# Projecting packed halves of the images with fp32r products, with a new order on all engines of a ViT tower kernel

## The reference, cut to what matters

```python
# x: (16 images, 64 channels, 256 positions, 4 heads) fp32
y = einsum('nclh,dc->ndlh', x, w) + b          # for q, k, v: D = 64, flattened to (n, 256, 256)
ew = exp(w_bias * local_mask)
num = einsum('ts,nsd->ntd', ew, exp(k) * v)
den = einsum('ts,nsd->ntd', ew, exp(k))
h = layernorm((sigmoid(q) * num / den) @ out_w + out_b + flatten(x)) * ln_g + ln_b
h = concatenate([cls_tok, h])                  # 257 rows per image
h = h + gated_recurrence(layernorm(h))         # gates r, i; scan along the rows; W_out
h = h + moe(layernorm(h))                      # shared FFN 256-1024-256 + top 2 of 8 experts
```

## Time and profile before

| | |
|---|---|
| runs | 1001.1, 1001.7, 1005.56 us (median 1001.7) |
| profiled execution | 1007.98 us, span 1006.3 us |
| mean granted TensorE clock | 0.961 |
| TensorE busy | 946.8 us (94%) |
| VectorE, ScalarE, GpSimd busy | 675.8, 458.2, 380.8 us |
| instructions | 21535 |

### The profile page before, as it was taken

The page is one execution under the profiler, slowest core; times in us unless marked ns, Lnnn a source line. Parts: engine busy times, 40 slices in busy tenths (PEclk is TensorE's granted clock), DMA queues, the critical chain, the costliest instruction groups (busy, mean ns, idle before and its releaser), DMA issues.

```text
span 1006.3 us, 21535 instructions
## 1 busy us (share of the span) xinstructions
PE 946.8 (94%) x6825; PEld 887.4 (88%) x6825; DVE 675.8 (67%) x2091; ACT 458.2 (46%) x1132; POOL 380.8 (38%) x470
## 2 busy tenths in 40 slices
PE   6979999999999999999886799999999999999996
PEld 4768899888898888898785799999999999999996
DVE  3588878887788877779777355654646456554643
ACT  2214344443444443444232355555555555555553
POOL 5282433333433424324524235342423435352322
PEclk9779999999999999999979799999999999999998
DMA  9315111001111001100013626473362825464222
GB/s 267 135 30 154 43 43 43 21 21 42 42 42 38 16 30 42 42 32 22 23 36 137 212 43 174 91 202 57 73 183 42 215 50 122 138 162 103 45 42 32
DMA packets 48163, 82.71 MB, mean 82 GB/s; under 512 B 6415, under 2 KB 30881, under 8 KB 48130
## 3 DMA queue, kind: packets, MB, share of 16 engines
q0 software_dynamic: 31056, 57.46, 23.7%
q1 hardware_dynamic: 17074, 24.83, 8.3%
HBM read 55.34 MB, written 26.96 MB: 82 GB/s over the span
## 4 chain that ended last, share of the span: by engine, by line
PE 60%; issue 19%; POOL 8%; DVE 7%; DMA 2%; ACT 1%; POOLq 1%; SPq 1%; DVEq 0%
PE ps_nd L755 17%; PE ps_proj L739 14%; PE ps_ri L739 6%; PE ps_nd L917 5%; PE ps_proj L822 5%; POOL out L700 5%; PE ps_ip L739 4%; PE ps_h L905 3%; PE ps_ip L890 2%; PE ps_t L829 2%; DMA R<-v_rows 1%; PE ps_t L1226 1%; DVE rden L1757 1%; DVE E L1750 1%; DVE yb L1984 1%
## 5 line engine op out<-in xcount | busy, mean ns | idle before, releaser
L1579 DVE TENSOR_TENSOR GL<-g_act,GH 128x256 fp32r<-128x256 f32 (+1 forms) x416 | 170.6, 423 | 169.8 <-ACT GH L1280 168.3
L1275 ACT ACTIVATE g_act<-ps_proj,fcb 128x256 f32<-128x256 f32 (+1 forms) x272 | 129.5, 476 | 284.9 <-PE ps_proj L739 264.0
L755 PE MATMUL ps_nd<-w2h,GH 128*128 128x256 f32 x832 | 240.9, 290 | 2.1 <-DVE GL L1579 2.1
L755 PE MATMUL ps_nd<-w2h,GL 128*128 128x256 f32 x832 | 233.9, 281 | 0.0
L755 PE MATMUL ps_nd<-w2l,GH 128*128 128x256 f32 x832 | 233.1, 280 | 0.0
L755 PEld LDWEIGHTS ps_nd<-w2h,GH 128*128 128x128 f32 x832 | 156.5, 188 | 6.3 <-issue 1.6
L1280 ACT CAST GH<-g_act 128x256 fp32r<-128x256 f32 (+1 forms) x416 | 161.0, 401 | 1.1
L755 PEld LDWEIGHTS ps_nd<-w2l,GH 128*128 128x128 f32 x832 | 157.1, 189 | 0.0
L755 PEld LDWEIGHTS ps_nd<-w2h,GL 128*128 128x128 f32 x832 | 156.5, 188 | 0.0
L739 PE MATMUL ps_proj<-xh,w1h 128*128 128x256 f32 (+1 forms) x544 | 127.8, 317 | 13.4 <-DVE E L1750 8.7
L700 POOL DMA_INDIRECT out<-yb,rows_to x72 | 115.5, 1605 | 16.7 <-issue 14.0
(11 more groups left out here) (263 smaller groups left out, 1844.1 us busy)
## 6 DMA issues: line engine op xcount, KB each, us to landing
R<-v_rows SPq DMA_DIRECT2D x37, 260.0 KB
w1h<-fc_w POOLq DMA_DIRECT2D x9, 1024.0 KB, 7.0
w2h<-pj_w POOLq DMA_DIRECT2D x9, 1024.0 KB, 9.8
stage<-fc_w POOLq DMA_DIRECT2D x9, 1024.0 KB, 11.7
stage<-pj_w POOLq DMA_DIRECT2D x9, 1024.0 KB, 14.0
v_rows<-tail_rows SPq DMA_DIRECT2D x16, 260.0 KB, 3.0
x<-x SPq DMA_DIRECT2D x16, 256.0 KB, 3.5
out<-yb SPq DMA_DIRECT2D x16, 256.0 KB, 2.2
```

The costliest lines, as they stand in the source:

```text
L755: last = pe.matmul(banks[a], g[:, j, a * P:(a + 1) * P], w[i][:, j, :], start=(j == 0 and q == 0), stop=(j == HT - 1 and q == 2))
L1275: act.activation(g_act[:, j % G_SLOTS, 0:width], banks[j % len(banks)][:, 0:width], ACT.Gelu_apprx_tanh, bias=fcb[i][:, j:j + 1]).then_inc ...
L1579: dve.tensor_tensor(GL[:, j, 0:width], g_act[:, j % G_SLOTS, 0:width], GH[:, j, 0:width].bitcast(F32), ALU.subtract).then_inc(gl_done, 1)
```

## The change

For images 2 to 15 the projection is computed from halves. x is laid out head by head as fp32r. `XA` has 128 rows: rows 0 to 63 the high part of x, rows 64 to 127 its low part. `XB` has 97 rows: the high part of x, then rows of ones. `WA` holds the high weights twice, `WB` the low weights, then zeros, then the high bias row. One product of XA with WA and one of XB with WB, accumulated in the bank, replace one fp32 product. ScalarE makes the high parts in two copies per image (`x_high`), VectorE the low part in one subtraction (`x_low`); SP loads x twice, into rows 0 to 63 and 64 to 127 of `X[par]`. XA, XB, WA, WB and `wproj_h` lie in buffers of expert 1's weights (`W1L[1]`, `W2L[1]`, `W1H[1]`, `W2H[1]`), so `next_weights` moves from step 2 to step 16 of GpSimd and waits for the last projection. Four loads (`pack_weights`), three copies (`pack_fill`) and one subtraction (`pack_split`) prepare the weights at the start.

Besides: `ranks` uses three products; the tails are written in step 18 of the mixer by SP, two blocks behind each list's end after image 14, and `rows_out` of image 15 waits for them; every engine but GpSimd and VectorE reads its limits before the experts' first block; eight products (`WARM`) stand before the first transpose of the experts, and `spare` adds 16 fp32 products in the start. The loop holds five pairs (images 4 to 13); steps 14 and 15 are written out as well, and the order of the calls is new in all written-out steps and in `step` of TensorE, ScalarE, VectorE and GpSimd.

```diff
+    KB = 97
-        X = [sb(f"x{i}", [KA, LH]) for i in range(2)]
+        X = [sb(f"x{i}", [P, LH]) for i in range(2)]
+        XA = [W1L[1][:].rearrange("p k n -> p (k n)")[:, i * LH:(i + 1) * LH] for i in range(2)]
+        XB = [W2L[1][:].rearrange("p j m -> p (j m)")[0:KB, i * LH:(i + 1) * LH] for i in range(2)]
+        WA = W1H[1][:, 0, :]
+        WB = W1H[1][0:KB, 1, :]
...
 load_x (SP)
-                after(sp, proj_ready, LT * (n - 1))
+                packed = not isinstance(n, int) or n >= 2
+                if isinstance(n, int) and n < 4:
+                    after(sp, proj_ready, LT * (n - 1))
+                else:
+                    sp.wait_ge(xs_done, n - 3)
                 sp.dma_start(X[par][0:C, :], x[n]).then_inc(x_loaded[par], 16)
+                if packed:
+                    sp.dma_start(X[par][C:2 * C, :], x[n]).then_inc(x_loaded[par], 16)
...
+            def tails(t, par):
+                sp.wait_ge(ends_ready, 1)
+                for e in range(NE):
+                    end = sp.value_load(ends_i[0:1, e:e + 1], min_val=e * LIST,
+                                        max_val=e * LIST + TOK - BLK)
+                    sp.dma_start(v_rows[bass.ds(end, 2 * BLK), :]
+                                 .rearrange("(b p a) m -> p b a m", b=2, a=2),
+                                 tail_rows[:].unsqueeze(1).to_broadcast([P, 2, 2, W])
+                                 ).then_inc(tails_stored, 16)
...
 GpSimd
+            def pack_weights(t, par):
+                flat_w = w_proj.rearrange("c h d -> c (h d)")
+                pool.dma_start(wproj_h, flat_w).then_inc(pack_loaded, 16)
+                pool.dma_start(WA[0:C, :], flat_w[0:C, :]).then_inc(pack_loaded, 16)
+                pool.dma_start(WA[C:2 * C, :], flat_w[0:C, :]).then_inc(pack_loaded, 16)
+                pool.dma_start(WB[KB - 1:KB, :], flat_w[C:KA, :]).then_inc(pack_loaded, 16)
             def next_weights(t, par):
+                pool.wait_ge(proj_ready, LT * NIMG)
             def step(t, par):
                 rstd_h(t, par)
                 affine(t, par)
+                rstd_u(t, par)
                 rstd_v(t, par)
-                rstd_u(t, par)
+                rows_out(t, par)
                 out_bias(t, par)
-                rows_out(t, par)
...
 project (TensorE)
                 for h in range(H):
-                    last = pe.matmul(ps_proj[:, h, :], head_view(par, lt, h), wproj[:, h, :],
-                                     start=True, stop=True)
+                    if packed:
+                        cols = slice(h * 4 * D, (h + 1) * 4 * D)
+                        pe.matmul(ps_proj[:, h, :], packed_view(XA[par], lt, h), WA[:, cols],
+                                  start=True, stop=False)
+                        last = pe.matmul(ps_proj[:, h, :], packed_view(XB[par], lt, h),
+                                         WB[:, cols], start=False, stop=True)
...
 ranks (TensorE)
-                for lt in range(LT):
-                    for k in range(lt + 1):
-                        pe.matmul(ps_rank[:, lt, :], (before_r if k == lt else ones_r)[:],
-                                  rmask[:, k, :], start=(k == 0), stop=(k == lt))
-                for k in range(LT):
-                    last = pe.matmul(ps_tot, ones_r[:], rmask[:, k, :], start=(k == 0),
-                                     stop=(k == LT - 1))
-                last.then_inc(rank_ready, 1)
+                pe.matmul(ps_count, ones_r[:], rmask_z[:].rearrange("p t e -> p (t e)"),
+                          start=True, stop=False)
+                pe.matmul(ps_count[:, 0:LT * NE], before_r[:],
+                          rmask.rearrange("p t e -> p (t e)"), start=False, stop=False)
+                pe.matmul(ps_tot, ones_r[:], rmask[:, 0, :], start=False, stop=True
+                          ).then_inc(rank_ready, 1)
...
+            def spare(t, par, k):
+                pe.wait_ge(consts, CONSTS)
+                for _ in range(2):
+                    pe.matmul(ps_ri[:, 1, :], ones_pp[:], zeros[:, 0, :], start=True, stop=True)
...
 step (TensorE)
                 hidden(t, par, 0)
+                hidden(t, par, 1)
                 sums0(t, par)
-                hidden(t, par, 1)
+                hidden(t, par, 2)
                 sums1(t, par)
-                hidden(t, par, 2)
                 hidden(t, par, 3)
+                hidden(t, par, 4)
                 turn_u(t, par)
-                hidden(t, par, 4)
+                hidden(t, par, 5)
                 rank(t, par)
-                hidden(t, par, 5)
+                hidden(t, par, 6)
                 gates0(t, par)
+                input0(t, par)
+                hidden(t, par, 7)
                 turn_v(t, par)
-                hidden(t, par, 6)
-                input0(t, par)
                 gates1(t, par)
...
 experts_tensor
+            limits = block_limits(pe)
+            for _ in range(WARM):
+                pe.matmul(ps_t[:, 0, :], ones_r[:], W2H[0][:, 0, :], start=True, stop=True)
             transpose_rows(0)
...
 ScalarE
+            def x_high(t, par):
+                n = t + 1
+                if live(n):
+                    p = 1 - par
+                    act.wait_ge(x_loaded[p], 16 * (n - p) + 16)
+                    if not isinstance(n, int) or n >= 4:
+                        act.wait_ge(proj_ready, LT * (n - 1))
+                    act.copy(XA[p].rearrange("c (h l) -> c h l", h=H),
+                             X[p][:].rearrange("c (l h) -> c h l", h=H)).then_inc(xq_done, 1)
+                    act.copy(XB[p][0:C, :].rearrange("c (h l) -> c h l", h=H),
+                             X[p][0:C, :].rearrange("c (l h) -> c h l", h=H)).then_inc(xq_done, 1)
 step (ScalarE)
                 gelu_j(t, par, 0)
                 gelu_j(t, par, 1)
                 high(t, par, 0)
+                x_high(t, par)
                 gelu_j(t, par, 2)
+                high(t, par, 1)
                 gelu_j(t, par, 3)
-                high(t, par, 1)
-                copy_u(t, par)
                 high(t, par, 2)
                 gelu_j(t, par, 4)
-                tanh0(t, par)
+                copy_u(t, par)
...
 VectorE
-                    if isinstance(n, int) and n == NIMG - 1:
-                        dve.wait_ge(run_ready, NIMG + 1)
+                    if isinstance(n, int) and n == NIMG - 2:
+                        dve.wait_ge(run_ready, NIMG)
                         dve.tensor_copy(ends_i[:], run[:]).then_inc(ends_ready, 1)
+            def x_low(t, par):
+                n = t + 1
+                if live(n):
+                    p = 1 - par
+                    dve.wait_ge(xq_done, 2 * (n - 1))
+                    low = XA[p][C:2 * C, :].rearrange("c (h l) -> c h l", h=H)
+                    dve.tensor_tensor(low, X[p][C:2 * C, :].rearrange("c (l h) -> c h l", h=H),
+                                      low.bitcast(F32), ALU.subtract).then_inc(xs_done, 1)
 step (VectorE)
                 ekv0(t, par)
                 h_sum(t, par)
+                ekv1(t, par)
                 h_norm(t, par)
-                ekv1(t, par)
...
                 u_norm(t, par)
-                ratio0(t, par)
-                u_low(t, par)
-                v_norm(t, par)
                 low(t, par, 0)
                 low(t, par, 1)
-                ratio1(t, par)
-                y_last(t, par)
+                v_norm(t, par)
+                u_low(t, par)
                 low(t, par, 2)
-                places(t, par)
+                ratio0(t, par)
                 low(t, par, 3)
                 low(t, par, 4)
+                ratio1(t, par)
+                places(t, par)
                 low(t, par, 5)
+                v_low(t, par)
                 low(t, par, 6)
+                x_low(t, par)
                 slots_out(t, par)
-                v_low(t, par)
+                y_last(t, par)
+                low(t, par, 7)
                 gate_a(t, par)
-                low(t, par, 7)
                 gate_b(t, par)
                 base_sum(t, par)
```

728 lines of the change are left out of this document (483 added, 245 removed).

## The result

The change makes the kernel slightly slower. Eight runs of the changed kernel have a median of 1011.2 us (1004.2 to 1017.9), beside 1006.1 us (1001.1 to 1006.9) of the kernel before on the same chip: ratio 1.0058, 95% interval 1.0032 to 1.0083. The forecast was 964 us, in a range of 944 to 986. The forecast was counted down from 1001.7 us, the median of three runs of the kernel before; the median of eight is 4.4 us higher, which would move the forecast by as much and no more. The profiled execution has a span of 1012.7 us, 6.4 more than the profiled one of before.

A forecast was written before the change was run, and what follows sets the result against it. TensorE, busy 94% of the span, was taken as the bound, with VectorE able to close in. Savings of 23 (twelve steps), 3 (start) and 12 (tail), 38 us, took the 1001.7 us median to 964 us; range 944 to 986.

The forecast's parts named there:

- the lower ends: Helper prices per image: x_high on ScalarE 2.24 of 2.24 to 3.7 us, x_low on VectorE 1.23 of 1.23 to 2.0.
- rival 1: Loop: added strided work becomes the bound, factor 1.65 on both helpers, 16 us over twelve steps, 980 us; chance 0.20.
- "nothing" for the load of x: SP queue: the second load of each x, 256 KB more per step, waits for x_low two images back; costs nothing.
- rows_out ahead of out_bias: GpSimd: the new order puts H0 off by 5 us, but v_sum wants it 8 us after next turn_y; costs nothing.
- the products: TensorE: 8 fp32r products replace each fp32 projection, 0.94 us together, saving 1.82 us per step; 2.05 with ranks.
- 28.9 us was laid out: Loop: one new step takes 28.9 us instead of 30.8, saving 1.9; twelve steps give 23 us.
- 3 faster forecast: Start: gains from projections and no next_weights, less spares and helpers; 3 us faster, between 8 slower and 12 faster.
- 12 forecast: Tail of the mixer: tails and limits moved earlier, next_low_second, new order of last steps; 12 us faster, between 5 and 20.
- stand in the wait for R: Tail: the eight WARM products cost nothing unless R is already there, then under 2 us.
- The 2.2 us for next_low_second: Tail: next_low_second leaves the stretch where it held VectorE's yb sum, worth 4.4 us, counted half: 2.2 us.
- Rival 4: Loop: strided reading costs ScalarE and VectorE factor 2.5, 4.3 us more per step, 52 in all, 1016 us; chance 0.04.
- signs for wrong: Copies of 1.9 us or more; hidden 4 or last ffn_out waiting over 1 us; GpSimd idle on a DMA; image 4 after 105 us.

The follow-up runs named there:

- e4: Changed kernel with input x laid out head by head by the host, so helpers and weight loads read at unit stride, all other work kept: 989.1 us median.
- e7: Changed kernel with SyncE issuing the load of image t+1 ahead of base_out(t): 6.7 us less than the changed kernel by the medians, ratio 0.9974.
- e8: Changed kernel with GpSimd adding out_bias ahead of rows_out in the loop's steps, as before the change: 2 us gained by the medians.
- e5: Changed kernel's order with the fp32 projection for all images, one load of x, no helpers or weight packing: ratio interval 0.9956 to 1.001 to the kernel before.
- e16: Changed kernel; from image 5 ScalarE gathers x once, halves and x_low read that copy packed; SyncE loads image t+1 early: 988.2 us, ratio 0.9862 to kernel before.
- e15: Changed kernel; from image 5 ScalarE gathers x once and halves and x_low read that copy packed; no early load: ratio interval 0.9939 to 1.0005 to kernel before.
- e9: Changed kernel with x_high and x_low packed in the order of x, TensorE's projection weight loads reading at a stride of 4 elements instead: 1015.6 us.
- e11: Changed kernel with both the head-by-head input of e4 and SyncE's early load of e7: 993 us.
- e10: e9 plus SyncE's early load of image t+1 ahead of base_out(t): worse still than e9, time not given.
- e13: Changed kernel; from image 4 ScalarE gathers x once into a free buffer, halves and x_low read that copy packed; no early load: 1014 us median.

## Why the prediction was wrong

**The step that failed is the pricing of x_high and x_low**: "I take the lower ends, since the same operation on the same engine is a nearer row than another engine's load or a reduction." The nearer row lacked the one property that decides, the stride. Both rows that had it said 1.6 to 1.65; measured are 1.95 on ScalarE and 1.65 on VectorE, 1.85 and 0.8 us more per image. The Trainium skill, "Advanced Engine Details and Errata", section "SBUF Cachelines", tells of a penalty where each access meets a different line; it pointed the right way, and these runs supply the price. The upper ends of the range, 3.7 and 2.0 us, were nearly right, but even they were taken too lightly: rival 1 had 16 us for them. The runs put the stride at 2.0 us a step between e4 and the changed kernel, and at 22 us by the medians (1011.2 against 989.1). That is about half of the miss: even with packed reads the kernel takes 989 us, above the range. Of the 44 us by which the profiled execution misses the sum, 22.5 lie in the twelve steps, 11.5 in the start and 11.4 in the tail, and the experts give 1.0 back; the points below have the rest.

**Second, "nothing" for the load of x.** "On SP nothing urgent is queued behind that wait, only base_out": the queue was read in one direction. base_out waits for VectorE's last operation of the step, and the next image's load is queued behind it. e7 gives it 1.0 us a step in the changed kernel, and 3.9 us in step 14. It cost nothing visible in e4's loop, where ScalarE and VectorE had room. The prediction also laid out one step and took it twelve times, and steps 14 and 15 have orders of their own.

**Third, rows_out ahead of out_bias: "nothing".** H0 was not late (in the ten steps VectorE waits 0.7 us in all for GpSimd, for rstd); but out_bias moved beside VectorE's sum, 1.95 us for 0.69 in four steps of ten. Undoing it moved the collision and gained 2 us by the medians (e8), no more than their spread.

**Right: the products.** A projection's 8 records stand 0.12 us apart (328.43 to 329.47 us, 1.04 in all where the sum had 0.94), the wider weights cost nothing, and with packed helpers the ten steps give 25.4 us in e4's profile where the sum had 19: 28.9 us was laid out and 28.3 came. The surplus fits the clock: before, every second step was at 0.95 and 1.5 us longer, in e4 none. The prediction took the pair's mean as given and did not ask whether it would change.

**Start: 3 faster forecast, 8.5 slower measured**, just past the bound of 8. The order alone has 4.8 of it (e5), and e4's start is 3 to 6 shorter than those of the changed kernel and its equals, which is the stride's part, the packed weight loads of images 0 and 1 included; both are near what equal starts differ by. VectorE and ScalarE have the chain there (start us, us, what):

```profile
31.36 1.98 ACT w2l L1561 x2
...
33.37 2.04 ACT w1l L1550
35.41 1.95 ACT w2l L1552
...
37.38 0.06 DVE w1l L2218
37.44 2.54 issue
39.98 1.22 DVE w1h L2225
41.20 0.67 DVE st L1821 x2
```

The "issue" here is x_low at work: its one operation runs from 37.38 us for 2.57. pack_fill, x_high, x_low and pack_split stand ahead of u_stats, which began at 36.57 us before and at 41.20 now. The prediction had these durations as VectorE's load and not as a chain.

**Tail: 12 forecast, 0.6 measured.** Tails left SyncE's path as said, and from the last sum to the experts' first product it is 12.6 us where it was 17.1. From the start of the tail to that sum it is 72.1 us where it was 68.1, which takes most of it back. What is late behind the sum was not only the last scatter:

```profile
555.36 0.69 DVE yb L2210
...
557.53 0.18 DVE bounds L2515
557.71 5.89 issue
563.60 2.07 PE ps_t L1396 x8
565.67 0.87 PE ps_t L1368 x4
```

VectorE writes the counts after its last sum, TensorE then takes 5.9 us to read eight limits (the prediction had 3.35 from the earlier trace rows, the part that stood on the chain there) and starts the WARM products at 563.60, while R had landed before 561.47, when VectorE copied from it (timeline):

```profile
561.47 0.17 DVE L2531 COPY info<-R 128x8 f32<-128x8 f32 x1 [0.89 <-DMA R<-v_rows]
```

That the WARM products "stand in the wait for R" was wrong: they lie behind the limits. In the same chain of before R was the last thing that the transposes waited for. The 2.2 us for next_low_second did not come either: it still holds a sum of yb, which is on the chain for 4.40 us where it was 5.08 (chain, and timeline of GpSimd):

```profile
540.15 4.40 DVE yb L2210
```

```profile
539.27 4.73 POOL L530 TENSOR_TENSOR w2l<-stage,w2h 128x1024 fp32r<-128x1024 f32 x2
```

By order alone the end gains 5.2 us (e5). In the changed kernel steps 14 and 15 take 3.9 us longer than in e5 and what follows up to the last sum 4.4, and that loses it again; how much of the 4.4 is the helpers isn't shown.

Of the rivals, rival 1, strided helpers at 1.65, had the mechanism and the step: 28.9 and 1.35 us make 30.25, and 30.3 came, though from 28.3 and 2.0. Its 980 us failed by steps 14 and 15, the start and the tail. Rival 4 had the sign and nearly the number (1016 us), at 0.04, but the number was luck: it asked for a factor "from 2.3", 1.65 and 1.95 came, and start, tail and the load's wait did the rest. The 0.04 came from asking for that mechanism alone to make up the whole difference. A slip beside it: by its own terms a gain under 0.5% needs a factor of 2.05, not 2.2 (33 us over twelve steps, 0.9 of cover, 3.47 of copies). Two of the signs for wrong came true, copies of 1.9 us or more and image 4 starting later than 105 us.

## What to carry to other kernels

Price an added pass by a row with its access pattern; where the rows with that pattern are of other engines, take their factor, not the packed time, and leave room above it (ScalarE had 1.95 where they said 1.65). In a saturated loop ask of each queue not only what waits behind the new instruction, but what the new instruction waits behind, through to the last operation of the step. A gather that several passes need is better done once and read packed afterwards: one fp32 gather on the engine with room and packed passes behind it, together with the early load (e16), turned a change of +0.6% into one of -1.4%; the gather without the early load (e15) had -0.3%.

## What the runs showed that was not expected

A copy of 1024 fp32 elements per partition at a stride of 16 bytes takes 2.05 us on ScalarE and 1.05 packed, whether for 128 partitions or 64; a subtraction on VectorE 2.02 and 1.22. A weight load at fp32r takes 325 to 329 ns at this stride (e9) and 197 packed, as at fp32 before, and in e9 this comes through to TensorE's step.

The granted clock falls to 0.50, the lower of its two levels (1.2 GHz), for some 3 us in a step, right after TensorE has idled 0.7 us ahead of hidden 0. Windows of the kernel before:

```profile
176.30:178.30 2.00, 1.32 (x7) 1.31 (x7) 1.74 (x5) 1.46 (x2) 1.92 (x2) 0.71 0.00 0
178.30:180.30 2.00, 2.00 (x5) 0.97 (x4) 1.68 (x14) 0.47 (x1) 0.96 (x3) 0.50 0.00 0
```

In the next step it idles as long at the same place and the clock stays at 1.00. A low step costs 1.3 to 1.5 us (e5 31.1 to 31.3 for 29.8, before 31.5 for 30.0). Which steps fall differs from variant to variant (none in e4, two in e11, nine in e10), and the spread of the variants' runs goes with it in part: in e7 994.0 us at a mean clock of 0.981 and 1008.6 at 0.970, in e13 1005.5 at 0.969 and 1018.5 at 0.962. What sets it off in one step and not in the next isn't settled.
